# A convolution in 4x28 patches, row transfers ahead of slabs and taps, and an Ln moved forward, in a two-layer image kernel on one core

## The reference, cut to what matters

```
layer 0:  h = depthwise conv 7x7 (x) + bias
          h = layernorm over the 96 channels of a pixel, gain, shift
          h = gelu(h @ w1 + b1) @ w2 + b2        (96 -> 384 -> 96)
          x1 = h * layer_scale + x
layer 1:  xs = silu(depthwise conv 5x5 (x1) + bias)        L = 56*56 pixels in a row
          dts, B, C = x_proj_w @ xs                        6 + 4 + 4 rows per image
          delta = softplus(dt_w @ dts + dt_b)              96 rows
          log_dA = max(delta * A[n], log 1e-9), n = 0..3
          P = exp(cumsum(log_dA))
          h[n] = P * cumsum(delta * B[n] * xs / max(P, 1e-9))
          y = sum over n of h[n] * C[n] + xs * D
```

## Time and profile before

| | us |
|---|---|
| median of the runs | 3910.67 |
| profiled execution, its own time | 3924.53 |
| its span, first to last instruction | 3922.7 |
| PE busy | 3536.6 (90%) |
| DVE busy | 3024.1 (77%) |
| ACT busy | 2570.0 (66%) |
| POOL busy | 2460.0 (63%) |
| mean granted clock of PE | 0.941 of full speed |

### The profile page before, as it was taken

How to read it: one execution, slowest core, us unless ns; L and a number is a source line. 1 busy time by engine, 2 the same in 40 slices (tenths; PEclk the granted TensorE clock), 3 DMA queues, 4 the chain that set the end, 5 groups by cost and what they waited for, 6 DMA issues and landing times.

```text
span 3922.7 us, 71069 instructions
## 1 busy us (share of the span) xinstructions
PE 3536.6 (90%) x22358; PEld 2662.2 (68%) x22358; DVE 3024.1 (77%) x3888; ACT 2570.0 (66%) x4292; POOL 2460.0 (63%) x2298
## 2 busy tenths in 40 slices
PE   6999999999999999997899898998989989899876
PEld 5878797978888797966766465565655656556422
DVE  3675847575675748473099899999999999999999
ACT  1462818274563718175588888788887888878865
POOL 0362716264452717173087888888888888888898
PEclk9999999999999999998899899998998989988888
DMA  7547474746556473525666465664756646565322
GB/s 220 174 123 231 97 255 99 231 115 194 165 137 211 97 259 96 194 64 127 167 170 178 129 180 141 167 181 122 192 149 164 183 123 189 149 166 162 103 79 62
DMA packets 383903, 613.00 MB, mean 156 GB/s; under 512 B 200064, under 2 KB 324320, under 8 KB 383216
## 3 DMA queue, kind: packets, MB, share of 16 engines
q1 hardware_dynamic: 383504, 607.96, 55.3%
HBM read 527.57 MB, written 80.28 MB: 155 GB/s over the span
## 4 chain that ended last, share of the span: by engine, by line
PE 33%; issue 8%; ACT 5%; POOL 4%; DVE 3%; DMA 1%; DVEq 0%; ACTq 0%; POOLq 0%; SPq 0%
PE ps_front L1315 11%; PE ps_y L1363 10%; PE ps_front L1308 4%; PE ps_prep L1337 3%; PE ps_y L1360 2%; PE ps_prep L1350 2%; PE ps_front L1328 2%; POOL h L1054 2%; DVE h L1140 1%; POOL u L1040 1%; ACT d_a L1226 1%; ACT d_a L1220 1%; DVE ps_q L1115 1%; POOL dxs L1028 1%; ACT xs L1184 1%
## 5 line engine op out<-in xcount | busy, mean ns | idle before, releaser
L322 POOL TENSOR_TENSOR h_low<-act_h,h_high 128x448 fp32r<-128x448 f32 x448 | 597.5, 1352 | 725.1 <-ACT h_high L521 724.8
L516 ACT ACTIVATE act_h<-ps_up,b 128x448 f32<-128x448 f32 x672 | 408.4, 633 | 729.2 <-PE ps_up L634 728.4
L1054 POOL TENSOR_TENSOR h<-h,c_rows 128x448 f32<-128x448 f32 x672 | 728.3, 1084 | 190.6 <-DVE h L1140 112.5
L1363 PE MATMUL ps_y<-h,ident 128*128 128x448 f32 x1344 | 689.9, 600 | 153.6 <-POOL h L1054 114.8
L1040 POOL TENSOR_TENSOR u<-dxs,b_rows 128x448 f32<-128x448 f32 x672 | 763.7, 1137 | 37.8 <-DMA bc_dram<-xd 21.7
L1115 DVE TENSOR_TENSOR_SCAN ps_q<-d_a,q_last,ps_q 128x450 f32<-128x450 f32 x576 | 661.5, 1148 | 1.3 <-ACT d_a L1226 1.3
L1140 DVE TENSOR_TENSOR_SCAN h<-d_a,h_last,ps_q 128x449 f32<-128x449 f32 x576 | 647.5, 1124 | 0.8 <-issue 0.7
L1315 PEld LDWEIGHTS ps_front<-win,taps 120*112 120x112 f32 x4608 | 535.2, 186 | 143.6 <-issue 141.0
L607 PE MATMUL ps_stage<-win,taps 124*112 124x112 f32 x6144 | 607.1, 260 | 2.7 <-DVE w_low L369 2.7
L607 PEld LDWEIGHTS ps_stage<-win,taps 124*112 124x112 f32 x6144 | 606.8, 178 | 3.2 <-DVE w_low L369 2.8
L1220 ACT ACTIVATE d_a<-delta,log_eps,a_neg 128x448 f32<-128x448 f32 x672 | 504.0, 751 | 97.4 <-DVE h L1140 55.8
(11 more groups left out here) (83 smaller groups left out, 6030.3 us busy)
## 6 DMA issues: line engine op xcount, KB each, us to landing
taps<-in_t_dram SPq DMA_DIRECT2D x192, 896.0 KB, 5.0
taps<-in_t_dram SPq DMA_DIRECT2D x192, 672.0 KB, 4.9
b_rows<-bc_dram SPq DMA_DIRECT2D x224, 224.0 KB, 3.0
c_rows<-bc_dram SPq DMA_DIRECT2D x224, 224.0 KB, 3.3
xres<-in_x_dram SPq DMA_DIRECT2D x224, 168.0 KB, 2.5
x_dram<-x1o SPq DMA_DIRECT2D x224, 168.0 KB, 2.0
x1pad<-x_dram SPq DMA_DIRECT2D x96, 392.0 KB, 5.8
out_dram<-y SPq DMA_DIRECT2D x168, 224.0 KB, 2.7
```

What stands on the lines that cost most here:

```text
L322: nc.gpsimd.tensor_tensor(h_low[u % 2][:, t, :], act_h[u % 2][:, t, :], h_high[u % 2][:, t, :], ALU.subtract).then_inc(h_low_ready[t], 1)
L516: nc.scalar.activation(act_h[u % 2][:, t, :], ps_up[t][:, 0:BT], ACT.Gelu, bias=b1[:, t:t + 1]).then_inc(gelu_done, 1)
L1054: nc.gpsimd.tensor_tensor(total, total, c_rows[n][:, :], ALU.mult).then_inc(hc_done, 1)
L1363: nc.tensor.matmul(total, ident[:, :], h[:, s % H_SLOTS, 0:BT], start=False, stop=(n == N - 1)).then_inc(y_added, 1)
```

## The change

1. The blocks of layer 1's convolution are patches of 4 rows x 28 columns. A window is 4 rows of 32 pixels, 128 partitions, and a channel takes KT2 = 2 matmuls, so a piece of a conv unit has 8 records. There are still 30 windows an image (15 in each half of the width). The matrices of taps are 448 KB a load for 672 KB.
2. x1 in DRAM is laid out in two halves with their borders, 56 rows x 32 pixels each, so that a slab is 448 KB in 2 runs of 7168 bytes for each of 32 partitions; before it was 392 KB in 56 runs of 224 bytes. For this layer 0's `residual` writes x1o in two instructions of 8 rows x 30 pixels, and the store has 192 runs of 1024 bytes in place of 96 of 1792. The outer borders are zeroed once, by four small memsets on POOL.
3. Back-transposes write each patch to its place in the band's pixel order; their number is the same.
4. On ACT the Ln of `softplus` stands first in its step, in front of `clip_a`, `keep_front` and `exp_a`.
5. On SP a load is issued at the later of AHEAD steps before its use and the step by which the schedule has freed its slot (`begin_at`), and after the step's xd, b, c and y transfers. The wait on `front_done` stays in front of it. For taps of the last five conv units that is three steps before their use.

```diff
-COLS2 = W + 2 * PAD2
-WIN2 = ROWS * COLS2
-KT2 = (ROWS + K2 - 1) // ROWS
-NWIN2 = (H + 2 * PAD2) // ROWS
+PATCH_ROWS, PATCH_COLS = 4, W // 2
+PCOLS = PATCH_COLS + 2 * PAD2
+SEEN = PCOLS - PAD2
+WIN2 = PATCH_ROWS * PCOLS
+KT2 = (PATCH_ROWS + K2 - 1) // PATCH_ROWS
+ROW_BLK = H // PATCH_ROWS
+ROW_WIN = (H + 2 * PAD2) // PATCH_ROWS
+NWIN2 = 2 * ROW_WIN
...
-                nc.vector.scalar_tensor_tensor(x1o[u % 2][:, :], ps_down[u % 2][0:C, 0:BT], b2[:, 0:1],
-                                               xres[u % 2][:, :], ALU.add, ALU.add).then_inc(x1_done, 1)
+                total = ps_down[u % 2][0:C, 0:BT].rearrange("c (h w) -> c h w", w=W)
+                res = xres[u % 2][:, :].rearrange("c (h w) -> c h w", w=W)
+                for f, seen in enumerate((slice(0, SEEN), slice(W - SEEN, W))):
+                    nc.vector.scalar_tensor_tensor(x1o[u % 2][:, f, :, PAD2 * (1 - f):PAD2 * (1 - f) + SEEN],
+                                                   total[:, :, seen], b2[:, 0:1], res[:, :, seen],
+                                                   ALU.add, ALU.add).then_inc(x1_done, 1)
...
-                sp.dma_start(xpad[rows, PAD2:PAD2 + H, PAD2:PAD2 + W],
-                             x1img[ds((f * GI + k % GI) * C + CB * (k // GI), CB), :, :]
-                             ).then_inc(slab_ready[k % SLABS], 16)
+                sp.dma_start(xpad[rows, :, PAD2:PAD2 + H, :].rearrange("c f h w -> c f (h w)"),
+                             x1[ds((f * GI + k % GI) * C + CB * (k // GI), CB), :, :, :
+                                ].rearrange("c f h w -> c f (h w)")).then_inc(slab_ready[k % SLABS], 16)
...
+            def begin_at(load, k, unit):
+
+                last_use = {load_slab: turn_unit, load_taps: conv_unit}[load]
+                slots, pieces = {load_slab: (SLABS, 1), load_taps: (SLOTS2, HALVES)}[load]
+                free = unit_step[last_use[k - slots]] + pieces + 1 if k >= slots else 0
+                return max(unit_step[unit] - AHEAD, free)
+
             def group(g, ahead, first=False):
 
-                todo = loads[SLABS:] if ahead else []
+                todo = sorted(loads[SLABS:], key=lambda load: begin_at(*load)) if ahead else []
                 for s in range(S):
                     b, j = s // STEPS, s % STEPS
                     f, fb = next_band(g, b)
                     if ahead == 2 and s == S - 2 * STEPS:
                         first_slabs(g + 2)
-                    while todo and unit_step[todo[0][2]] <= s + AHEAD:
-                        load, k, _ = todo.pop(0)
-                        load(g + 1, False, k)
...
                     if s >= N + Y_LAG + 1 and (s - N - Y_LAG - 1) % N == 0:
                         store(g, (s - N - Y_LAG - 1) // N)
+                    while todo and begin_at(*todo[0]) <= s:
+                        load, k, _ = todo.pop(0)
+                        load(g + 1, False, k)
...
+                    if (more or b + 1 < BANDS) and j - 1 in Z_AT:
+                        softplus(f, fb, Z_AT.index(j - 1), True)
                     if more or ahead < S:
                         clip_a(g, ahead)
...
-                        if j - 1 in Z_AT:
-                            softplus(f, fb, Z_AT.index(j - 1), True)
...
-                                win[cb % 2][:, k * CQ + c, :, w:w + IMG_BLK],
+                                win[cb % 2][:, k * CQ + c, :, :].rearrange("p i (f r) -> p (i f) r",
+                                                                           f=2)[:, :, w:w + ROW_BLK],
```

53 lines of the change are left out of this document (34 added, 19 removed).

## The result

The changed kernel takes 3896.59 us, median of eight runs (3873.52 to 3903.02), against 3910.89 us for eight runs of the kernel before: 0.9949 of it, 95% interval 0.9929 to 0.9969. The gain is 14 us where 69 were forecast.

| part of the span | before | after | difference | forecast |
|---|---|---|---|---|
| start to the end of layer 0 | 1814.15 | 1848.52 | +34.4 | +10 |
| end of layer 0 to the first scan | 146.4 | 125.0 | -21.4 | -20 |
| first scan to the end | 1962.2 | 1927.7 | -34.5 | -58.7 |

A forecast was written before the change was run, and what follows sets the result against it. PE was taken to bound the first layer and DVE the second. Steady part -52.7, first group -6, early stretch -20, residual +10 make -69 us from 3924.5, so 3856; off the runs' median 3842, own range 3828 to 3858.

The forecast's parts named there:

- C: Steps 65 to 67 of a group, behind step 60's back-transposes: DVE's waits of 27.3 us become 5.4, saved 21.9.
- Row transfers ahead on SP: On SP, row loads go before slabs and taps: all 38.0 us of DVE's waits for u taken as gone.
- A: Steps 7 to 9, behind step 0's back-transposes: DVE's waits of 33.4 us in six groups become 16.8, saved 16.6.
- The Ln first: On ACT, the Ln comes 2.0 us earlier with a copy in the step, 1.3 without.
- Two taps for three: Conv pieces from 1.29 to 0.86 us, 21 us a group; z 1.8 to 2.1 us earlier at B and C.
- B: Step 43, behind step 35's back-transposes (in two groups also step 19): all 14.2 us of z_log waits saved.
- The stretch before the first scan: Constants, 16 conv and turn pairs and eight convs before the first scan: saved 20 us, bounds 8 and 28.
- The residual in two: Layer 0: second DVE instruction adds 0.16 us a unit, at most 96 of 224 units see it; loss 10 us.
- The rule weighed: Trainium skill: matmuls stay fast back to back, slow behind waits; it speaks against cutting 21 us of PE work a group.
- clock: Rival, chance 0.10: gaps in PE bring half of the slow pieces to B and C; 20 us of gain go, 3862.
- backlog stays: Rival, chance 0.15: with u in time DVE stands the same time for z_log; steady 52.7 us falls to 15, 3884.
- The signs of being wrong: Wrong if the group's period stays above 242 us, PE waits for taps, or the first layer grows by over 20 us.

The follow-up runs named there:

- e4: The kernel before with only SP's new order (row transfers first, loads when their slot is free): 1.0000 of before.
- e7: The kernel before with the Ln first and SP's new order, without patches: 0.9927 of before.
- e3: The kernel before with only the Ln moved to the front of its step: 0.9915 of before, 3884.56 us.
- e8: The changed kernel with SP's order put back, so patches and the Ln first: 0.9923 of before.
- e14: The changed kernel, SP's new order too, with layer 0 as before and the halves laid out by the slab's transfer: 0.9875 of before.
- e13: The changed kernel with SP's order put back, layer 0 as before, and the slab's transfer laying out the halves in runs of 120 bytes: 0.9888 of before.
- e6: The changed kernel with useless matmuls on PE in a group's last ten steps and inside the burst of step 0: 1.0021 of before.
- e9: The changed kernel with SP's order put back; in layer 0 DVE adds only the bias, POOL adds the input and lays out halves, store in 96 runs: 1.0282 of before.

## Why the prediction was wrong

Point by point, by its own steps:

- *What bounds it*: right. DVE sets the pace of layer 1, and the three places were read rightly. (The waits for z_log are 36.9 of 74.9 us by the earlier trace rows, a half and not a third.) Of the causes, the one given for C, slabs in pieces of 224 bytes, was wrong (e4).
- *Row transfers ahead on SP*: the waits for u went to 0 as forecast, but as a gain it failed: alone it is worth 0.0% (e4), with the Ln nothing that can be measured (e7 against e3), nor with the patches (after against e8, e14 against e13). The sum at A, "3.59 us earlier, the wait is 2.8 for 3.59 + 1.31", holds only with the Ln's 2 us in it; the saving at A is the Ln's: A's 33.4 us are 34.0 with SP's order alone, 23.2 with the Ln alone and 21.4 with both.
- *The Ln first*: right: 30 us alone (0.9915), the largest net gain of the three parts. It leaves 14.0 us of z_log's waits, and 34.1 of those for u.
- *Two taps for three*: a piece takes 0.90 us (1.80 for two) for the forecast 0.86; B and C are empty: forecast 14.2 + 21.9 saved, measured all 41.4, of which the patches can do 30 alone and the Ln 16 alone. This part was right.
- *A, steady part*: the step that failed first. Forecast 16.8 us left in six groups, measured 50.0. It took A to be untouched by the patches, with PE's wait of 5.45 us at the turn, "which stays", and PE's pace behind it as before. With patches that pause is two, and in four of six groups PE ran on at 1.2 GHz long after it. In the group at 0.73 the forecast was nearly right, 3.3 us and a period of 238.0; at 0.77 the wait was 4.8 us and the period 238.7. Six groups at 238 would be 1428 us, they took 1455.8: 28 us that go with the slow starts.
- *The stretch before the first scan*: right, -21.4 for -20. *The first group*: its period 242.4 to 235.4, -7 for -6.
- *The residual in two*: the second step that failed. Its price was exact (0.16 us a unit); "only 96 of 224 units see it, loss 10" was not: 19 to 24 us reach the end. *The store at nothing* was the third: 16 us.
- *The rule weighed*: the rival "clock" was the right mechanism in the wrong place. I had it bring waits back to B and C, where the burst's pieces are; it struck A, at the loop's turn, and cost some 28 us for the 20 given to it. The rival "backlog stays" holds for SP's part.
- *The signs of being wrong*: two of the three came true, a mean period of six groups above 242 (242.6) and a first layer longer by over 20 us (34).

By stretches the miss is: forecast -69, plus 24 for layer 0 (34 for 10), less 1 for the early stretch, plus 25 for the six groups (1455.8 us where 52.7 less than before's 1483.4 is 1430.7), less 1 for the first group, is -22; the profiled executions show -21.5. Counted by waits, the six groups have 33 us more at A than forecast and 5 fewer at C. The rivals were each given alone; what happened is the clock and a dearer layer 0 at once, and their sum lay beyond the range. The medians of the runs show 14 us of gain and the two traces 21.5; after's second trace, with more slow starts, took 3919.87 us.

What stays open: why a PE that is busy without a gap is granted 1.2 GHz for 6 us after one turn of the loop and for over 40 us after another, in kernels with patches often and without them in one start of 30. Two things differ with patches, the second pause inside the burst and less work of PE in the steps before the turn, and neither was tried by itself: the filling of e6 covers both. And the way from the store's 192 runs to PE is not seen in full.

## What to carry to other kernels

Cost an instruction added to an engine that is not the bound by what the bound waits for it in the trace, and if the bounding engine already waits for it in two lines, take most of the price, not the part that the schedule seems to expose. Put a change of layout where the queue has room: the same patches cost 34 us in the layer that PE bounds, and as short runs in layer 1 some 8 us before the first scan and 17 us more of waits for u (e13 beside e8), by the medians that way is 14 us faster. When two waits follow each other on one engine, removing the first was worth nothing, alone (e4) or with the Ln (e7); here one moved line gave at least as much as the whole change. And before a wait is named as the proof of a cause, see when the engine came to it: in e6 the wait at step 7 shrank because DVE was late.

## What the runs showed of the hardware

- A store of 96 partitions takes SP 0.33 us to issue with 96 runs and 0.58 with 192, and lands in 2.0 to 2.2 us or 2.7 to 2.8; 14% more bytes in the same number of runs add 0.2 us at most.
- POOL takes 0.83 us to add 96 x 240 float32 into a strided tile; DVE's residual over 96 x 240 takes 0.45 us.
- DVE's multiply over 112 x 672 float32 takes 0.86 us with POOL idle, 1.49 us on average in after, and 2.43 us beside POOL's additions of e9.
- After its waits at the end of a group PE was granted 1.2 GHz for 17 us in one group of after and for 55 us in another, with the same instructions in both.
- The mean granted clock and the time of one kernel go together: over twelve more runs of after 0.922 to 0.924 goes with 3900 to 3920 us, 0.933 to 0.936 with 3872 to 3884. Before has it too: over the 17 runs beside them 0.938 goes with 3932.2 us and 0.950 with 3901.8. A fixed schedule on all engines doesn't make a fixed time.
